# A hand-ordered Perceiver block on one core: the fourth tile's retention projections moved between the heads of the first batch's retention

## The reference

```python
x = x + xattn(layernorm(x), ctx, ctx, mask, ...)   # 16 heads, 4096 keys
x = x + retention(layernorm(x), Wq, Wk, Wv, Wg, Wo, gnorm_w)
x = x + experts(layernorm(x), gate_w, gate_b, expert_w, expert_b)  # 8 experts
```

```python
q, k = apply_rotary(x @ Wq.T, x @ Wk.T)            # 4 heads of 64
v = x @ Wv.T ; g = x @ Wg.T                        # 4 heads of 128
o = (q k^T * decay) v                              # causal, decay gamma_h ** (i - j)
o = o * rsqrt(mean(o * o over a head) + eps) * gnorm_w
o = o * (g * sigmoid(g))
return o @ Wo.T
```

## Time and profile before

| | |
|---|---|
| median of 3 runs | 241.67 us |
| the three runs | 239.74, 241.67, 241.96 us |
| the profiled execution's own time | 239.15 us |
| its span, first to last instruction | 237.2 us |
| PE busy | 215.2 us, 91% of the span |
| DVE busy | 154.4 us, 65% |
| ACT busy | 111.5 us, 47% |
| mean granted TensorE clock | 0.995 of full |

### The profile page before, as it was taken

One profiled execution on the slowest core, in us unless ns is written; L12 is line 12 of the kernel. 1 busy time (PEld: TensorE's weight loads), 2 busy tenths in 40 slices (PEclk: granted clock), 3 DMA queues, 4 the chain that ended last, 5 costly groups with the idle time before them and its releaser, 6 DMA issues.

```text
span 237.2 us, 3690 instructions
## 1 busy us (share of the span) xinstructions
PE 215.2 (91%) x1314; PEld 115.7 (49%) x1314; DVE 154.4 (65%) x352; ACT 111.5 (47%) x238; POOL 36.6 (15%) x45
## 2 busy tenths in 40 slices
PE   8799997889799999999998989988988998899892
PEld 8367543344454544444443535445746754544340
DVE  6793888954928479787880346585184728585682
ACT  3227855575557487878889664233242051101000
POOL 8006998204503100000000000000000000000000
PEclk9999999999999999999999999999999999999998
DMA  5699673777099000920000000000000000000000
GB/s 182 216 228 322 191 199 94 190 185 260 14 237 221 4 1 3 284 73 3 3 3 1 0 3 1 0 0 0 3 0 0 0 4 1 0 0 22 23 26 26
DMA packets 15391, 17.93 MB, mean 76 GB/s; under 512 B 2600, under 2 KB 14472, under 8 KB 15368
## 3 DMA queue, kind: packets, MB, share of 16 engines
q1 hardware_dynamic: 14072, 17.30, 25.9%
q10 hardware_dynamic: 1296, 0.34, 0.8%
HBM read 9.79 MB, written 0.52 MB: 43 GB/s over the span
## 4 chain that ended last, share of the span: by engine, by line
PE 60%; DVE 16%; DMA 6%; ACT 5%; POOL 5%; issue 4%; SPq 3%; POOLq 0%; DVEq 0%; ACTq 0%
PE bank L826 10%; PE bank L811 10%; PE bank L1010 8%; PE bank L751 7%; PE bank L917 6%; DVE cneg L1592 4%; PE bank L990 3%; PE bank L878 3%; PE bank L711 3%; DMA ctxT<-in_ctxT 3%; DMA mask_all<-in_mask 2%; ACT prob L1269 2%; PE bank L698 2%; SPq L400 2%; PE bank L898 2%
## 5 line engine op out<-in xcount | busy, mean ns | idle before, releaser
L1592 DVE TENSOR_REDUCE cneg<-bank 128x1 f32<-128x896 f32 x64 | 68.1, 1087 | 24.2 <-PE bank L751 23.4
L1269 ACT ACTIVATE prob<-bank 128x512 f32<-128x512 f32 x112 | 65.6, 597 | 24.2 <-PE bank L811 21.7
L811 PE MATMUL bank<-qstack,kstack 100*128 100x256 bf16 x224 | 42.3, 274 | 3.4 <-ACT prob L1269 2.0
L751 PE MATMUL bank<-kstack,qstack 97*128 97x448 bf16 x128 | 34.7, 353 | 3.1 <-DVE cneg L1592 3.0
L826 PE MATMUL bank<-prob,vals 128*32 128x256 f32 x448 | 35.8, 391 | 0.4 <-ACT prob L1269 0.4
L811 PEld LDWEIGHTS bank<-qstack,kstack 100*128 100x128 bf16 x224 | 17.3, 97 | 31.6 <-ACT prob L1269 15.6
L917 PE MATMUL bank<-w_late,xnT 128*128 128x512 f32 x48 | 22.0, 595 | 0.3 <-ACT xnT L1298 0.3
L1010 PE MATMUL bank<-ctxT,xnT 128*128 128x512 f32 x32 | 17.1, 616 | 0.3 <-DVE x_in L1773 0.3
L1773 DVE SCALAR_TENSOR_TENSOR x_in<-bank,nwts,x_in 128x256 f32<-128x256 f32 x32 | 15.5, 484 | 2.5 <-PE bank L1010 1.4
L1010 PE MATMUL bank<-kpart,xnT 128*128 128x512 f32 x32 | 16.3, 592 | 0.0
L751 PEld LDWEIGHTS bank<-kstack,qstack 97*128 97x128 bf16 x128 | 11.5, 98 | 8.9 <-DVE cneg L1592 4.2
(11 more groups left out here) (151 smaller groups left out, 260.2 us busy)
## 6 DMA issues: line engine op xcount, KB each, us to landing
kstack<-kpart SPq DMA_DIRECT2D x24, 224.0 KB
w_late<-in_w_ret SPq DMA_DIRECT2D x1, 1536.0 KB
mask_all<-in_mask SPq DMA_DIRECT2D x2, 512.0 KB, 5.1
ctxT<-in_w_exp SPq DMA_DIRECT2D x1, 1024.0 KB
kpart<-in_w_exp SPq DMA_DIRECT2D x1, 1024.0 KB
ctxT<-in_ctxT SPq DMA_DIRECT2D x2, 448.0 KB, 5.5
ctxT<-in_ctxT SPq DMA_DIRECT2D x1, 896.0 KB, 7.4
qstack<-acc SPq DMA_DIRECT2D x12, 64.0 KB, 3.0
```

Source lines behind the costliest of these rows:

```text
L751: mm = pe.matmul(out, qstack[0:MROW + 1, h, b, qt * P:(qt + 1) * P], kstack[0:MROW + 1, b, h, half_ * HC:(half_ + 1) * HC], start=True, st ...
L811: mm = pe.matmul(out[:, hh * NQ:(hh + 1) * NQ], kstack[0:KROWS, b, h, kt * P:(kt + 1) * P], qstack[0:KROWS, h, b, :], start=(hh == 0 or no ...
L1269: act.activation(prob[:, n % PROBS, :], bank[:, S0 + jj, :], ACT.Exp).then_inc(c["prob_ready"], 1)
L1592: dve.tensor_reduce(cneg[:, st % 2, i:i + 1], bank[:, pair:pair + 2, 0:HC], AXXY, ALU.max, negate=True).then_inc(c["max_read"], 1)
```

## The change

On PE the three projections of tile 3 no longer stand behind batch 0's heads: the first stands behind `ret_scores(1)`, the second behind `ret_scores(3)`, the third behind `ret_values(3)`. On ACT `take_v(3)` moves ahead of the eight squares. On DVE the two rope products of tile 3 move between the second and the third decay, and its `rope_first` and `rope_second` move from inside the Newton rounds to ahead of `norm_and_gate(0)`. No instruction is added or removed, and no DMA moves.

```diff
                 ret_scores(0)
-                for r in range(1, RH):
-                    ret_scores(r)
-                    ret_values(r - 1)
-                ret_values(RH - 1)
-                for m in range(3):
-                    project_ret(TT - 1, m)
+                ret_scores(1)
+                project_ret(TT - 1, 0)
+                ret_values(0)
+                ret_scores(2)
+                ret_values(1)
+                ret_scores(3)
+                project_ret(TT - 1, 1)
+                ret_values(2)
+                ret_values(3)
+                project_ret(TT - 1, 2)
                 turn_qk(TT - 1)
...
                 take_qk(TT - 2)
+                take_v(TT - 1)
                 squares_of(0)
                 squares_of(1)
-                take_v(TT - 1)
                 gate(TT - 1)
...
-                for r in range(RH):
-                    decay_weights(r)
+                decay_weights(0)
+                decay_weights(1)
                 rope_products(TT - 1)
-                norm_and_gate(0, [lambda: rope_first(TT - 1), lambda: rope_second(TT - 1)])
+                decay_weights(2)
+                decay_weights(3)
+                rope_first(TT - 1)
+                rope_second(TT - 1)
+                norm_and_gate(0)
```

## The result

The changed kernel takes 243.37 us (median of 12 runs, 241.81 to 248.97) against 240.66 us for the kernel before (12 runs, 239.39 to 242.92). The ratio is 1.0117, 95% interval 1.0086 to 1.0147: slower by 1.2%. The forecast was +0.9 us, "the same, on the slow side", 242.5 us with a range of 239.7 to 243.5. The measured median lies in the range, but the size is off by a factor of three, and the loss just passes the 1% to which I gave 0.08.

The account below looks back on a forecast made before the run. PE was busiest (91% of the span), but batch 0's chain over heads, squares, norm and y decided: +2.73 -0.97 -0.67 = +1.09 at y, about +0.9 in all, so 240.05 us (242.5 on the median), range 239.7 to 243.5.

Parts of the forecast that it names:

- PE's order: On PE, two projections (3.46 us) less the gap of 0.73 us end batch 0's heads 2.73 us later.
- Squares, norm, y: In batch 0's retention: later heads +2.73, rope products -0.97, rotation -0.67, so y +1.09 us; turn_y(1) +0.88, taken as +0.9.
- What is late next, and no slack in the tail: From retention_out to the program's end each stage hangs on the one before, so nothing takes the 0.9 us back.
- the prediction's own sign of being wrong: The forecast would be wrong if the tail after turn_y(1) were shorter or longer than before by over 0.3 us.
- The cause of the gap: PE's 0.74 us gap before batch 0's first values matmul: DVE's first decay late because gate_product(2) held it until 164.83.
- Rival C: PE's clock halves behind two gaps before retention_out(0): +4.2 us, with the 0.9 +5.1, 246.8 us; chance 0.04.
- rival D: Decay 2 or 3 late, or squares slower beside PE: up to +2.0 us, 243.7, still within 1%; chance 0.10.
- -0.7 for the changed order: PE's filled 0.74 us gap stays won, with y not waited for: 238.4 us, or 241.0 on the median; chance 0.10.

## Why the prediction was right in part and wrong in size

- **PE's order: right.** Two projections ahead of the last head less the gap, +2.73. In the trace the first square moved by 173.27 - 170.59 = 2.68. The switches between projections and heads cost nothing. The kernel with three ahead repeats the term, +1.72 for 1.73.
- **Squares, norm, y: right.** L1726 at 175.48 (forecast 175.52), y at 177.70 (177.75), `turn_y(0)` at 178.88 (178.93), `turn_y(1)` at 180.47 (180.45). The forecast +0.9 is +0.77 when both traces are counted from the first scores. Putting the rotation back cost 0.67, as the sum had it.
- **What is late next, and no slack in the tail: right.** From head 4 to the end the changed kernel takes 240.0 - 186.92 = 53.08 us, before 237.2 - 184.33 = 52.87. But the prediction's own sign of being wrong, a tail behind `turn_y(1)` longer by over 0.3 us, is there: 240.0 - 180.47 = 59.53 for 237.2 - 179.57 = 57.63, 1.90 more, nearly all of it in `retention_out(0)`.
- **The cause of the gap: wrong, at no cost.** I wrote that DVE was late because `gate_product(2)` held it. The kernel with the decays first shows that the decay had nothing to read earlier. The four records of L955 for heads 0 and 1 start within 0.3 us of each other and the four of L957 within 0.1, so head 0's scores end about when head 1's do. The filling of the gap didn't depend on its cause.
- **Rival C: this is the step that failed.** I had its mechanism and place, forecast the gaps at 1.1 and 1.2 (1.08 and 1.50), and priced it at +4.2 for 4.20 us of PE work at half speed (measured 1.70 and 3.06: in the first profile the clock was back at 1.00 from 184.53, before the 4.20 us were over). So the size was some way too high; what made the forecast wrong is the chance, 0.04. I let one execution speak against it: PE idle for 1.41 us at 61.89 with a full clock. Whether such a gap costs the clock differs from execution to execution, so one trace excludes nothing. The kernel with the decays first has the same PE order as before and the same gap, and there the clock fell:

```profile
62.15 0.55 PE L751 MATMUL bank<-kstack,qstack 97*128 97x448 bf16 x2 [1.41 <-DVE cneg L1592]
...
64.00:66.00 2.00, 2.00 (x8) 1.28 (x8) 0.67 (x2) 1.11 (x3) 0.00 (x0) 0.50 0.05 12
```

For the retention all profiles agree: with a gap of 1.5 us or more left there, the eight records of `retention_out(0)` take 3.36 to 3.62 us in all five (the changed kernel twice, `take_v` behind, rotation inside, first gap filled); with the gap ahead of `turn_y(0)` filled they take 1.89 in all three. The runs point the same way. With such a gap left, 40 of 41 lie at a mean clock of 0.991 or less (12 + 6 of the changed kernel, 6 with `take_v` behind, 5 with the rotation inside, 11 of 12 with the first gap filled). With it filled it is 7 of 34 (0 of 12, 3 of 11, 4 of 11), and in the kernel before 42 of 86. The spread of the four times of before, 239.15 to 241.96, was a hint of the same that I took for noise.

- **The range held by luck.** Its upper end, 243.5, was made of the highest run of before and part of rival D, a norm or heads disturbed by other engines, and nothing of that kind happened. The start of the sum was luck too: the median of three runs, 241.67, was 1.0 us above the 240.66 of the twelve. From 240.66 the order alone gives 241.5; the rest of the 243.37 is rival C, which I had priced at 246.8, outside the range.
- **The clock and the pages.** The clock fell behind a stretch in which PE was busy for 0.92 of 3.43 us, and with fillers in the same place it stayed full. The Trainium skill (TensorE: Matmul & The Clock Gate, What's actually happening) says that the clock follows how busy PE has lately been; by it rival C was due more than 0.04, and the trace agrees: 0.52 of full from 181.10 to 184.53. The Trainium skill (Perfetto Trace Analysis, Optimization Strategy) says that interleaving regimes with different busiest engines may help; I had read it as -0.7 for the changed order, and the trace disagrees: +0.77 us at `turn_y(1)`. With one projection moved 0.85 us were won, and by its trace nearly all of that is the shorter norm (0.70 at y), not work pulled forward on PE.

Open: how the chance of a fall grows between a gap of 0.74 us (one fall in a profile, no difference between filled and unfilled runs) and 1.50 (nearly always), and where the kernel before loses its clock in half of its runs. The gap at 62 us is one place, by the trace above, but filling it left the two groups. Splitting the squares by head, so that they start before the last head, wasn't tried; the heads of a tile share a bank, so ACT would read one that PE is still writing.

## What to carry to other kernels

When PE work moves ahead of other PE work, ask what the displaced work releases on the other engines. Here two projections (3.46 us of work) went ahead of the last head to fill 0.73 us of idling, and pushed squares and norm back by 2.7 us. One projection paid, because it delayed the squares by 0.94 us only, which the norm had spent waiting for DVE's rope products before. Then add up the gaps that the new order makes. A PE gap of 1.5 us cost its own length and, in all five profiles that have it in the retention, a fall of the clock behind it, worth another 1.7 to 3.1 us where it was measured; ten useless matmuls won back 1% of the program. One profile with a full clock doesn't show that a gap is harmless: look at the mean clock of a dozen runs, and then at a profile for the place, since the mean doesn't tell it.

## What was unexpected of the hardware

Ten useless matmuls made the program 1% faster (1.0117 to 1.0011). The fall came behind the gap, not in it: clock 1.00 while PE was busy for 0.92 of 3.43 us, then 0.52 while it was busy for 3.41 of 3.43. And the scores of two heads, issued one after the other, whose operands lie in different halves of the 128 partitions (64 each), ran together: in the changed kernel both took 0.86 us to the next matmul's start (163.91 to 164.77), where one head alone takes 0.85 (167.35 to 168.20).
